# Second graph attention layer: exponentials as the stationary operand, h streaming, normalised straight from PSUM

## The chip, the cores and the metric

The kernel runs on one core of one Trainium2 chip. The metric is device time in microseconds; the kernel before took 1403.1 us (median of three runs, 1400.07 to 1413.15). Its matmuls run on TensorE, its elementwise work on VectorE, ScalarE and GpSimd, its transfers are issued mostly by SyncE. TensorE's clock is granted at one of two levels, 2.4 GHz (1.00 in the profile) or 1.2 GHz (0.50).

## The reference, cut to what matters

Four layers follow each other with residual sums: a diffusion over a graph, a top-2 mixture of experts, two graph attention layers (GAT) in a row, and a top-1 mixture of experts. The attention layers are what matters here: 1024 nodes, 8 heads, 128 channels per head in the first and 64 in the second.

```python
def gat_conv(x, src, dst, W, att_src, att_dst, bias, heads, out_ch):
    N = x.shape[0]
    h = (x @ W).reshape(N, heads, out_ch)
    a_src = jnp.einsum('nhc,hc->nh', h, att_src)
    a_dst = jnp.einsum('nhc,hc->nh', h, att_dst)
    e = jax.nn.leaky_relu(a_src[src] + a_dst[dst], NEG_SLOPE)
    m = jax.ops.segment_max(e, dst, num_segments=N)
    ex = jnp.exp(e - m[dst])
    s = jax.ops.segment_sum(ex, dst, num_segments=N)
    alpha = ex / (s[dst] + 1e-16)
    msg = h[src] * alpha[:, :, None]
    out = jax.ops.segment_sum(msg, dst, num_segments=N)
    return out.reshape(N, heads * out_ch) + bias
...
h = gat_conv(x, src, dst, W1, att_src1, att_dst1, b1, HEADS, nhid)
h = jax.nn.relu(h)
out = gat_conv(h, src, dst, W2, att_src2, att_dst2, b2, HEADS, ncls)
return jax.nn.log_softmax(out, axis=1)
```

## The kernel before, in words

One function, `attend`, writes both attention layers; `final` is true for the second. The graph is dense here: `CT` holds, for each tile of 128 source nodes and all 1024 destinations, the logarithm of the number of edges. A head is worked off in eight source tiles. One head `hd` with one source tile `s` is a pair, `k = 8 * hd + s`, 64 pairs in all. Four engines each run over the pairs in their own written order and meet by semaphores:

- GpSimd adds `CT` and a row `qb` into `am`, a ring of four tiles of 128x1024 (L1461).
- ScalarE forms a relu of 128x1024 in PSUM banks 4 and 5, `RELU` (`relu`, L1474), which VectorE adds to `am` (`counted`, L1574). `RELU` is held once, so relu `k + 1` waits until VectorE has added relu `k`.
- ScalarE takes the exponential of `am` into `PT` (`exp`, L1481), again a ring of four. In its loop relu `k + 1` stands ahead of exponential `k`.
- TensorE sums the messages of the pair into PSUM. `h` has a column of ones behind the channels of each head, so that the sum of the exponentials comes out as a last column or row.
- Between the pairs VectorE takes maxima over the neighbours of each node for two or three heads ahead (`maxed`, L1568), out of a row of scores that TensorE spreads over banks 6 and 7 (`a_row`); the table `A_ROW` sets the pair ahead of which each stands. TensorE waits there for the maxima of the head before.
- Between the pairs TensorE also makes the rest of the projection `h = x W`, in ten parts set by `H_AFTER`: behind pairs (0,1), (0,3), (1,1), (1,5), (2,1), (2,5), (3,5), (4,1), (4,5), (5,1), written (head, tile). ScalarE moves each out of PSUM three pairs later (`H_MOVED`). There is none behind (5,1).

The first layer sums with `gather` (L1688): for each of eight blocks of destinations the 128x128 exponentials are the stationary operand and `h` of one head, 129 columns, streams. The result has destinations on partitions. VectorE normalises at the next head's tile 0, right behind `counted`: `normed` waits for the eight sums, adds 1e-16, takes reciprocals (L1583, L1585) and multiplies bank by bank (L1599); the next head's first gather waits for it bank by bank. TensorE then turns the result for the second layer (`turned`).

The second layer before sums with `columns` (L1701): `h`, 65 columns, is stationary, and the exponentials stream in two matmuls of 512. The result has channels on partitions, in banks 0 and 1. ScalarE copies it to `oT` (`moved`, L1488) at tile 0 of the next head, TensorE turns it by eight transposes into banks 2 and 3 (`rows`, L1712) at tile 2, and VectorE normalises it into `zo` (L1596) at tile 4. The next head's first `columns` waits for the copy. After the last head come bias and log-softmax. Each fp32 matmul stands as two records in the trace, a transpose as one.

Of the kernel before, what the change touches and what calls it, by code (L numbers as in the profile page):

```python
# [5 lines left out]
ALU = mybir.AluOpType  # L6
ACT = mybir.ActivationFunctionType
F32 = mybir.dt.float32
# [8 lines left out]
P = 128  # L17
KIB = 1024
# [5 lines left out]
def build(nc, ins, out):  # L24

    x_d, src_d, dst_d = ins["x"], ins["src"], ins["dst"]
    N, D = x_d.shape
# [19 lines left out]
    with ctx:  # L47
# [16 lines left out]
        def place(name, shape, dt, at):  # L64

            return nc.alloc_sbuf_tensor_at(name, shape, dt, offset=BASE + at)
# [1259 lines left out]
        def attend(tag, KI, CH, xT, W, W_d, v, h, bias_d, adr, qdr, final):  # L1326
# [4 lines left out]
            NBK = -(-NT // PER)  # L1331
            SLOPE = 1 / NEG_SLOPE
            PAIRS = HEADS * NT
            EVS = 1 if final else NBK

# [10 lines left out]
            def h_units(hd, s):  # L1348

                if hd < HEADS // 2:  # L1350
# [5 lines left out]
            EARLY = 5  # L1356
            FIRST = {0: ((1, 5),), 1: ((1, 6),), 2: ((1, 7),), 3: ((2, 0), (2, 1)), 4: ((2, 2), (2, 3)),
                     5: ((2, 4), (2, 5)), 6: ((2, 6), (2, 7)), 7: ((3, 0),)}
            LATER = ({0: (1,), 1: (2,), 2: (3,), 3: (4,), 5: (5, 6), 6: (7,)} if final else
                     {1: (1,), 2: (2,), 3: (3,), 4: (4, 5), 5: (6,), 6: (7,)})  # L1360

            def maxima(hd, s):
                if hd == 0:
# [12 lines left out]
            if final:  # L1376
                bias = place(tag + "_bias", [P, F], F32, 16 * KIB)
                zo = place(tag + "_zo", [P, NT, F], F32, 129 * KIB)
                zt = place(tag + "_zt", [P, 2, F], F32, 18 * KIB)
                oT = place(tag + "_oT", [CH + 1, N], F32, 201 * KIB)  # L1380
            s_ad, s_qb = [sem(f"{tag}_ad{j}") for j in range(2)], [sem(f"{tag}_qb{j}") for j in range(2)]
            s_w = [sem(f"{tag}_w{j}") for j in range(2)]
            s_q0, s_q0m = sem(tag + "_q0"), sem(tag + "_q0_moved")
# [11 lines left out]
            with nc.Block() as block:  # L1395
# [71 lines left out]
                def _(act):  # L1467
# [13 lines left out]
                        act.activation(PT[:, k % PR, :], am[:, k % RING, :], ACT.Exp, bias=as02[:, s, hd:hd + 1],  # L1481
                                       scale=1 - NEG_SLOPE).then_inc(s_exp, 1)

                    def moved(hd):
                        act.wait_ge(s_O, NT * hd + NT)

                        wait(act, s_tr, hd)
                        act.copy(oT[:], PS[0:CH + 1, 0:2, :].rearrange("p a n -> p (a n)")).then_inc(s_oT, 1)  # L1488

                    def out(hd, half):  # L1490
                        act.wait_ge(s_tr, 2 * hd + half + 1)
                        act.activation(x2T[:, hd, half * 512:(half + 1) * 512], PS[:, 3, :], ACT.Relu,
# [36 lines left out]
                    for k in range(PAIRS):  # L1529
                        hd, s = k // NT, k % NT  # L1530
                        if k + 1 < PAIRS:
                            relu(k + 1)
                        exp(k)
                        if (hd, s) in H_MOVED:
                            h_moved(H_MOVED[hd, s], 3)
                        if final and s == 0 and hd:
                            moved(hd - 1)
                        if not final and s == 6 and hd:
                            out(hd - 1, 0)
                        if not final and s == 1 and hd >= 2:  # L1540
                            out(hd - 2, 1)
                    if not final:
                        out(HEADS - 2, 1)
                        out(HEADS - 1, 0)
                        out(HEADS - 1, 1)
                    else:
                        moved(HEADS - 1)
                        for t in range(NT):
                            act.wait_ge(s_z, t + 1)
                            act.activation(zt[:, t % 2, :], zo[:, t, :], ACT.Exp, bias=nmt[:, t:t + 1],  # L1550
                                           accum_out=sq[:, t:t + 1]).then_inc(s_ze, 1)
                            act.wait_ge(s_ze, t + 1)
                        act.activation(ve[:], sq[:], ACT.Ln).then_inc(s_ln, 1)

                @block.vector
                def _(dve):
# [17 lines left out]
                        dve.tensor_tensor(am[:, k % RING, :], RELU, am[:, k % RING, :], ALU.add).then_inc(s_all, 1)  # L1574

                    def normed(hd):
                        if final:
                            dve.wait_ge(s_tr, hd + 1)
                        else:
                            dve.wait_ge(s_O, NT * hd + NT)  # L1580
                        bank = 2 if final else 0
                        O = PS[:, bank:bank + NBK, 0:PER * (CH + 1)].rearrange("p b (t c) -> p b t c", c=CH + 1)
                        link(dve.tensor_scalar(dn[:, 0:NBK * PER].rearrange("p (b t) -> p b t", t=PER), O[:, :, :, CH],  # L1583
                                               1e-16, None, ALU.add), 2 * hd + 1)
                        link(dve.reciprocal(rd[:, 0:NBK * PER], dn[:, 0:NBK * PER]), 2 * hd + 2)  # L1585
                        scale = rd[:, 0:NBK * PER].rearrange("p (b t) -> p b t", t=PER).unsqueeze(3).to_broadcast(
                            [P, NBK, PER, CH])
                        if final:
                            dst = zo[:, :, hd * CH:(hd + 1) * CH]
                        else:  # L1590

                            wait(dve, s_tr, 2 * hd)
                            dst = o1[:, 0:NBK * PER, :]
                        dst = dst.rearrange("p (b t) c -> p b t c", t=PER)
                        if final:
                            dve.tensor_tensor(dst, O[:, :, :, 0:CH], scale, ALU.mult).then_inc(s_ev, 1)  # L1596
                        else:
                            for b in range(NBK):
                                dve.tensor_tensor(dst[:, b, :, :], O[:, b, :, 0:CH], scale[:, b, :, :], ALU.mult  # L1599
                                                  ).then_inc(s_ev, 1)  # L1600

                    dve.wait_ge(s_b, 1)
                    dve.tensor_copy(ab[:].rearrange("p t h -> p (t h)"), PS[:, 3, 0:NT * 2 * HEADS]).then_inc(s_bm, 1)
# [6 lines left out]
                    for k in range(PAIRS):  # L1610
                        hd, s = k // NT, k % NT
                        counted(k)
                        if hd and s == (4 if final else 0):
                            normed(hd - 1)
                        for ahead, t in maxima(hd, s):
                            maxed(ahead, t)
                    normed(HEADS - 1)
                    if final:

                        dve.wait_ge(s_ev, HEADS * EVS)  # L1620
                        dve.wait_ge(s_bias, 16)
                        n = 2 * HEADS
                        for t in range(NT):
# [13 lines left out]
                def _(pe):  # L1637
# [53 lines left out]
                                           stop=(s == NT - 1 and d in (NT - 1, *range(PER - 1, NT, PER))))  # L1691
                        mm.then_inc(s_O, 1)

                    def columns(hd, s):

                        if s == 0:
                            wait(pe, s_oT, hd)
                        h_ready(hd, s)
                        pe.wait_ge(s_exp, NT * hd + s + 1)
                        for half in range(2):  # L1700
                            mm = pe.matmul(PS[0:CH + 1, half, :], h[:, s, hd, :],  # L1701
                                           PT[:, (NT * hd + s) % PR, half * 512:(half + 1) * 512], start=(s == 0),
                                           stop=(s == NT - 1))
                        mm.then_inc(s_O, 1)

                    def rows(hd, moved):
                        pe.wait_ge(s_oT, hd + 1)
                        wait(pe, s_ev, hd)

                        wait(pe, s_hm, moved)  # L1710
                        for d in range(NT):
                            mm = pe.transpose(PS[:, 2 + d // PER, (d % PER) * (CH + 1):(d % PER + 1) * (CH + 1)],  # L1712
                                              oT[:, d * P:(d + 1) * P], ident[0:CH + 1, 0:CH + 1])
                        mm.then_inc(s_tr, 1)

                    def turned(hd, half, moved):
                        pe.wait_ge(s_ev, EVS * (hd + 1))
                        wait(pe, s_xm, 2 * hd + half)

                        pe.wait_ge(s_hm, moved)  # L1720
                        for d in range(NT // 2):
                            mm = pe.transpose(PS[:, 3, d * P:(d + 1) * P], o1[:, half * NT // 2 + d, :], ident[:])
                        mm.then_inc(s_tr, 1)
# [23 lines left out]
                    for k in range(PAIRS):  # L1747
                        hd, s = k // NT, k % NT
                        if k in A_ROW:
                            a_row(A_ROW[k])  # L1750
                        columns(hd, s) if final else gather(hd, s)
                        if (hd, s) in H_AFTER:
                            wait(pe, s_hm, H_AFTER[hd, s])
                            if final:
                                wait(pe, s_ev, hd if s > 2 else hd - 1)
                            else:
                                wait(pe, s_xm, turns)
                            h_tile(H_AFTER[hd, s], 3)
                        if final and s == 2 and hd:
                            rows(hd - 1, h_before(hd, s))  # L1760
                        if not final and s in (3, 7) and hd:
                            turned(hd - 1, s // 7, h_before(hd, s))
                            turns += 1
                    if final:
                        rows(HEADS - 1, 2 * NT)
                    else:
                        turned(HEADS - 1, 0, 2 * NT)
                        turned(HEADS - 1, 1, 2 * NT)

# [85 lines left out]
```

## Time and profile before

| | us |
|---|---|
| median of three runs | 1403.1 |
| the profiled execution | 1406.6 |
| its span | 1404.9 |
| TensorE busy in the span | 1075.2 (77%) |
| VectorE busy | 761.8 (54%) |
| ScalarE busy | 514.6 (37%) |
| GpSimd busy | 594.8 (42%) |
| mean granted clock of TensorE | 0.871 |

The second attention layer's pairs run from about 1010 to 1215 us of the span, those of the first layer from 752 to 957. Two records of a group of instructions can overlap, so a group's busy time is not its count times its mean. What an engine waited for stands behind its idle time, as "idle <-engine tile line" of the instruction that released it. The first attention layer runs the same code with the gathers that the change puts into the second, which makes its rows a second source of durations.

### The profile page before, as it was taken

The page shows a single profiled execution, that of the slowest core. Times are in us where ns is not written, and L with a number is a line of the kernel's source. Part 1 is how long each engine was busy: PE and PEld are TensorE (multiplying, and loading weights), DVE is VectorE, ACT ScalarE, POOL GpSimd, SP SyncE. Part 2 cuts the span into 40 slices and gives each one's busy share as a digit, 9 for nine tenths or more (in the row PEclk, how much of TensorE's full clock was granted, in tenths as well). Part 3 has the DMA queues.
Part 4 walks back from the last instruction along what each step waited for, and adds up shares of the span by engine and source line. Part 5 has one row for each costly group of instructions (what it writes and reads, how often), then busy time and mean ns, then how long its engine had stood idle before and what let it go on. Part 6 is the DMA issues. An engine that isn't in the chain of part 4 may idle for free. (4 is left out here: it accounts for less than half of the span.)

```text
span 1404.9 us, 17550 instructions
## 1 busy us (share of the span) xinstructions
PE 1075.2 (77%) x5484; PEld 740.1 (53%) x5488; DVE 761.8 (54%) x1609; ACT 514.6 (37%) x710; POOL 594.8 (42%) x471
## 2 busy tenths in 40 slices
PE   3999379650999999968398888878887887533696
PEld 2444367550777777747246777763644342132463
DVE  6888465636333333333638777751777675653134
ACT  2333433220111111101236676772466667630010
POOL 1000645105555555443026876781576777402002
PEclk9999699855999999975589999999999999855796
DMA  3000000073699999643030111101011111003974
GB/s 101 0 1 0 1 0 0 1 255 122 202 298 300 303 304 302 200 148 113 0 92 16 46 46 31 46 16 65 28 45 31 45 43 40 0 9 108 336 253 158
DMA packets 112476, 144.28 MB, mean 103 GB/s; under 512 B 30184, under 2 KB 72776, under 8 KB 112408
## 3 DMA queue, kind: packets, MB, share of 16 engines
q1 hardware_dynamic: 96168, 118.47, 26.1%
q0 software_dynamic: 14080, 21.03, 4.5%
q10 hardware_dynamic: 2160, 3.93, 0.7%
q8 instruction: 35, 0.57, 0.2%
q14 instruction: 33, 0.27, 0.1%
HBM read 138.71 MB, written 29.81 MB: 120 GB/s over the span
## 5 line engine op out<-in xcount | busy, mean ns | idle before, releaser
L1461 POOL TENSOR_TENSOR am<-CT,qb 128x1024 f32<-128x1024 f32 x128 | 299.3, 2363 | 61.7 <-ACT PT L1481 37.3
L1574 DVE TENSOR_TENSOR am<-PS,am 128x1024 f32<-128x1024 f32 x128 | 156.6, 1223 | 74.8 <-ACT PS L1474 67.1
L1474 ACT ACTIVATE PS<-adb,ab 128x1024 f32<-128x1024 f32 x128 | 142.9, 1117 | 90.5 <-DVE am L1574 90.4
L1042 DVE COPY yo<-PS 128x512 f32<-128x512 f32 x79 | 54.7, 692 | 208.9 <-PE PS L980 200.6
L1568 DVE CUSTOM_DVE_ANT_0 masked<-PS,mask 128x1024 f32<-128x1024 f32 x128 | 156.1, 1220 | 19.0 <-issue 17.3
L972 PE MATMUL PS<-xgT,w1r 128*128 128x128 f32 x1264 | 155.7, 277 | 0.0
L1007 ACT ACTIVATE hT<-PS,b1T 128x128 f32<-128x128 f32 x158 | 49.5, 364 | 288.4 <-PE PS L972 250.7
L1688 PE MATMUL PS<-h,PT 128*128 128x129 f32 x1024 | 128.3, 282 | 33.0 <-ACT PT L1481 26.4
L972 PEld LDWEIGHTS PS<-xgT,w1r 128*128 128x128 f32 x1264 | 149.2, 194 | 1.2 <-issue 1.2
L980 PE MATMUL PS<-w2r,hT 128*128 128x512 f32 x316 | 148.6, 593 | 0.1
L1481 ACT ACTIVATE PT<-am,as 128x1024 f32<-128x1024 f32 x128 | 145.2, 1134 | 0.3 <-DVE am L1574 0.3
L1688 PEld LDWEIGHTS PS<-h,PT 128*128 128x128 f32 x1024 | 122.7, 196 | 41.7 <-issue 40.5
L1701 PE MATMUL PS<-PT,h 128*65 128x512 f32 x256 | 124.9, 620 | 23.5 <-ACT PT L1481 14.3
L914 POOL DMA_INDIRECT ys_scratch<-yo,r_rowsi x64 | 65.6, 1025 | 109.0 <-DVE yo L1042 98.8
L351 DVE TENSOR_SCALAR oh_src<-iota,eT 128x1024 f16 x164 | 78.8, 480 | 17.7 <-PE PS L479 11.4
L1033 DVE COPY xgT<-PS 128x512 f32<-128x512 f32 x79 | 53.9, 683 | 54.6 <-PE PS L963 52.1
L1701 PEld LDWEIGHTS PS<-PT,h 128*65 128x65 f32 x256 | 32.9, 140 | 95.7 <-issue 79.4
L963 PEld LDWEIGHTS PS<-ident,xg 128*128 128x128 f32 x316 | 39.6, 145 | 67.6 <-issue 32.8
L980 PEld LDWEIGHTS PS<-w2r,hT 128*128 128x128 f32 x316 | 54.1, 191 | 39.2 <-issue 38.7
L479 PE MATMUL PS<-oh_src,oh_dst 128*128 x328 | 73.5, 379 | 0.9 <-DVE oh_dst L353 0.3
L909 POOL DMA_INDIRECT xg<-xs_scratch,r_rowsi x64 | 65.0, 1015 | 21.2 <-issue 20.3
L172 PE MATMUL PS<-ident,xln 128*128 128x128 f32 x96 | 20.5, 389 | 66.3 <-DVE xln L153 65.9
(308 smaller groups left out, 1601.2 us busy)
## 6 DMA issues: line engine op xcount, KB each, us to landing
w1r<-in_L_ffn_W SPq DMA_DIRECT2D x79, 512.0 KB, 6.2
w2r<-in_L_ffn_W SPq DMA_DIRECT2D x79, 512.0 KB, 7.6
adb<-a_scratch SPq DMA_DIRECT2D x16, 512.0 KB, 4.1
qb<-q_scratch SPq DMA_DIRECT2D x14, 512.0 KB, 3.7
wc<-in_L_gnn_W SPq DMA_DIRECT2D x16, 256.0 KB
xg<-xs_scratch SPq DMA_DIRECT2D x15, 256.0 KB
ys_scratch<-yo ACTq DMA_DIRECT2D x15, 256.0 KB
x_res<-in_x SPq DMA_DIRECT2D x1, 2048.0 KB, 10.5
```

The source lines that it names most:

```text
L351: dve.tensor_scalar(oh_src[:, bass.ds(slot, 1), c, :], iota[:], eT[:, 0, c, bass.ds(q, 1)], None, ALU.is_equal)
L479: mm = pe.matmul(PS[:, 2 * (t % 2) + h, :], oh_dst[:, bass.ds(slot, 1), c, :], oh_src[:, bass.ds(slot, 1), c, h * 512:(h + 1) * 512], star ...
L914: pool.indirect_dma_start(ys[0:rows, :], bass.IndirectOffsetOnAxis(picked[:, e:e + 1], 0), yo[:, e % 4, :], None, bounds_check=rows - 1, o ...
L972: mm = pe.matmul(PS[:, 2 + j % 2, c * P:(c + 1) * P], w1r[:, j, k, c * P:(c + 1) * P], xgT[:, j % 2, k, :], start=(k == 0), stop=(k == KD ...
L980: mm = pe.matmul(PS[:, 4 + j % 2, :], hT[:, j % 2, c, :], w2r[:, j, c, :], start=(c == 0), stop=(c == HC - 1))
L1461: pool.tensor_tensor(am[:, k % RING, :], CT[:, s, :], qb[:, hd % 2, :], ALU.add).then_inc(s_sum, 1)
L1474: act.activation(RELU, adb[:, hd % 2, :], ACT.Relu, bias=ab[:, s, hd:hd + 1]).then_inc(s_relu, 1)
L1481: act.activation(PT[:, k % PR, :], am[:, k % RING, :], ACT.Exp, bias=as02[:, s, hd:hd + 1], scale=1 - NEG_SLOPE).then_inc(s_exp, 1)
L1568: dve.tensor_tensor_reduce(masked[:], ASB, mask[:, t, :], 1.0, -3.0e38, ALU.subtract, ALU.max, mrow[:, hd % 2, t:t + 1]).then_inc(s_max, 1)
L1574: dve.tensor_tensor(am[:, k % RING, :], RELU, am[:, k % RING, :], ALU.add).then_inc(s_all, 1)
L1688: mm = pe.matmul(PS[:, d // PER, (d % PER) * (CH + 1):(d % PER + 1) * (CH + 1)], PT[:, (NT * hd + s) % PR, d * P:(d + 1) * P], h[:, s, hd, :],
L1701: mm = pe.matmul(PS[0:CH + 1, half, :], h[:, s, hd, :], PT[:, (NT * hd + s) % PR, half * 512:(half + 1) * 512], start=(s == 0), stop=(s == ...
```

## The change

In the second layer too, TensorE uses `gather`, so with 16 records of 65 columns for a pair in place of 4 of 512; `columns`, `rows` and ScalarE's `moved` are gone with their buffer `oT`. VectorE's `normed` reads banks 0 and 1 straight, at tile 0 of the next head, and writes `zo` in two products instead of one; the maxima that stood at tile 0 stand where the first layer has them. The projections (`h_tile`) no longer wait for the normalisation.

```diff
-            EVS = 1 if final else NBK
...
-            LATER = ({0: (1,), 1: (2,), 2: (3,), 3: (4,), 5: (5, 6), 6: (7,)} if final else
-                     {1: (1,), 2: (2,), 3: (3,), 4: (4, 5), 5: (6,), 6: (7,)})
+            LATER = {1: (1,), 2: (2,), 3: (3,), 4: (4, 5), 5: (6,), 6: (7,)}
...
-                    def moved(hd):
-                        act.wait_ge(s_O, NT * hd + NT)
-
-                        wait(act, s_tr, hd)
-                        act.copy(oT[:], PS[0:CH + 1, 0:2, :].rearrange("p a n -> p (a n)")).then_inc(s_oT, 1)
...
-                        if final and s == 0 and hd:
-                            moved(hd - 1)
...
                     def normed(hd):
-                        if final:
-                            dve.wait_ge(s_tr, hd + 1)
-                        else:
-                            dve.wait_ge(s_O, NT * hd + NT)
-                        bank = 2 if final else 0
+                        dve.wait_ge(s_O, NT * hd + NT)
+                        bank = 0
...
-                        if final:
-                            dve.tensor_tensor(dst, O[:, :, :, 0:CH], scale, ALU.mult).then_inc(s_ev, 1)
-                        else:
-                            for b in range(NBK):
-                                dve.tensor_tensor(dst[:, b, :, :], O[:, b, :, 0:CH], scale[:, b, :, :], ALU.mult
-                                                  ).then_inc(s_ev, 1)
+                        for b in range(NBK):
+                            dve.tensor_tensor(dst[:, b, :, :], O[:, b, :, 0:CH], scale[:, b, :, :], ALU.mult
+                                              ).then_inc(s_ev, 1)
...
-                        if hd and s == (4 if final else 0):
+                        if hd and s == 0:
                             normed(hd - 1)
...
-                    def columns(hd, s):
-
-                        if s == 0:
-                            wait(pe, s_oT, hd)
-                        h_ready(hd, s)
-                        pe.wait_ge(s_exp, NT * hd + s + 1)
-                        for half in range(2):
-                            mm = pe.matmul(PS[0:CH + 1, half, :], h[:, s, hd, :],
-                                           PT[:, (NT * hd + s) % PR, half * 512:(half + 1) * 512], start=(s == 0),
-                                           stop=(s == NT - 1))
-                        mm.then_inc(s_O, 1)
-
-                    def rows(hd, moved):
-                        pe.wait_ge(s_oT, hd + 1)
-                        wait(pe, s_ev, hd)
-
-                        wait(pe, s_hm, moved)
-                        for d in range(NT):
-                            mm = pe.transpose(PS[:, 2 + d // PER, (d % PER) * (CH + 1):(d % PER + 1) * (CH + 1)],
-                                              oT[:, d * P:(d + 1) * P], ident[0:CH + 1, 0:CH + 1])
-                        mm.then_inc(s_tr, 1)
...
-                        columns(hd, s) if final else gather(hd, s)
+                        gather(hd, s)
                         if (hd, s) in H_AFTER:
                             wait(pe, s_hm, H_AFTER[hd, s])
-                            if final:
-                                wait(pe, s_ev, hd if s > 2 else hd - 1)
-                            else:
+                            if not final:
                                 wait(pe, s_xm, turns)
                             h_tile(H_AFTER[hd, s], 3)
-                        if final and s == 2 and hd:
-                            rows(hd - 1, h_before(hd, s))
...
-                    if final:
-                        rows(HEADS - 1, 2 * NT)
-                    else:
+                    if not final:
                         turned(HEADS - 1, 0, 2 * NT)
                         turned(HEADS - 1, 1, 2 * NT)
```

On TensorE, from the last score row on (L1656 before, L1638 after, for head 7, in head 4), the first eight rows before (L1701 `columns`, L1673 projections, L1712 transposes; the counts are matmuls):

```order
L1656 MATMUL PS<-a_6351,sel 128x512 x2
L1701 MATMUL PS<-PT,h_8616 65x512 x2
L1673 MATMUL PS<-W2t_8618,x2T 128x128 x16
L1701 MATMUL PS<-PT,h_8616 65x512 x8
L1673 MATMUL PS<-W2t_8618,x2T 128x128 x16
L1701 MATMUL PS<-PT,h_8616 65x512 x2
L1712 MATMUL PS<-ident,a_oT 128x65 x8
L1701 MATMUL PS<-PT,h_8616 65x512 x16
```

and after, up to the end of the layer (L1670 gathers, L1655 projections):

```order
L1638 MATMUL PS<-a_6351,sel 128x512 x2
L1670 MATMUL PS<-h_8616,PT 128x65 x8
L1655 MATMUL PS<-W2t_8618,x2T 128x128 x16
L1670 MATMUL PS<-h_8616,PT 128x65 x32
L1655 MATMUL PS<-W2t_8618,x2T 128x128 x16
L1670 MATMUL PS<-h_8616,PT 128x65 x176
```

Behind the last projection nothing but gathers of 65 columns stands in TensorE's row, 176 of them, which are 22 pairs; before, matmuls of 512 columns and transposes stood there.

On VectorE, the last maximum (made in head 5) and what follows up to the end of head 6, before (L1574 is `counted`, L1583, L1585 and L1596 are `normed`):

```order
L1568 ISA masked,mrow<-PS,mask 128x1024
L1568 ISA mrow 128x1
L1574 TENSOR_TENSOR am<-PS,am 128x1024 x6
L1583 TENSOR_SCALAR dn<-PS 128x8
L1585 RECIPROCAL rd<-dn 128x8
L1596 TENSOR_TENSOR a_zo<-PS,rd 128x8x64
L1574 TENSOR_TENSOR am<-PS,am 128x1024 x8
```

and after (L1562 is `counted`, L1568, L1570 and L1581 are `normed`):

```order
L1556 ISA masked,mrow<-PS,mask 128x1024
L1556 ISA mrow 128x1
L1562 TENSOR_TENSOR am<-PS,am 128x1024 x2
L1568 TENSOR_SCALAR dn<-PS 128x8
L1570 RECIPROCAL rd<-dn 128x8
L1581 TENSOR_TENSOR a_zo<-PS,rd 128x4x64 x2
L1562 TENSOR_TENSOR am<-PS,am 128x1024 x8
```

The normalisation of head 5 has moved from behind six sums to behind two, that is from the fifth sum of head 6 to its first, and its product is made in two halves.

## Rows read from the trace of the kernel before

**Rows 1.** Second layer by head: stretch, length, busy time (records) per engine, clock
```profile
1036.60:1066.40 29.80, 24.21 (x106) 12.46 (x106) 21.63 (x39) 19.20 (x20) 25.70 (x16) 0.94 0.15 36
...
1096.10:1121.00 24.90, 19.34 (x75) 8.40 (x74) 19.98 (x35) 18.70 (x18) 18.33 (x13) 1.00 0.14 43
...
1150.80:1175.40 24.60, 18.97 (x73) 8.03 (x72) 16.08 (x26) 18.49 (x18) 14.95 (x11) 1.00 0.12 39
1175.40:1195.80 20.40, 15.74 (x40) 4.41 (x40) 10.77 (x12) 18.30 (x18) 17.68 (x9) 1.00 0.15 44
1195.80:1215.10 19.30, 15.54 (x40) 4.48 (x40) 8.75 (x10) 15.25 (x15) 12.71 (x6) 1.00 0.00 0
```

**Rows 2.** Timeline, second layer: start, duration, what, idle before it
```profile
1066.49 1.01 ACT L1488 COPY a_oT<-PS 65x1024 f32<-65x1024 f32 x1 [3.06 <-PE PS L1701]
...
1068.62 1.22 DVE L1574 TENSOR_TENSOR am<-PS,am 128x1024 f32<-128x1024 f32 x1 [5.75 <-ACT PS L1474]
...
1071.47 3.73 PE L1673 MATMUL PS<-W2t,x2T 128*128 128x128 f32 x32
...
1178.85 1.12 ACT L1474 ACTIVATE PS<-adb,ab 128x1024 f32<-128x1024 f32 x1 [0.29 <-DVE am L1574]
...
1181.33 1.12 ACT L1474 ACTIVATE PS<-adb,ab 128x1024 f32<-128x1024 f32 x1 [0.29 <-DVE am L1574]
```

**Rows 3.** Timeline, end of the second layer's last head
```profile
1211.50 3.62 PE L1701 MATMUL PS<-PT,h 128*65 128x512 f32 x8 [0.58 <-ACT PT L1481]
...
1216.21 0.71 PE L1712 MATMUL PS<-ident,a_oT 65*128 65x65 f32 x8 [1.10 <-ACT a_oT L1488]
...
1217.40 0.69 DVE L1596 TENSOR_TENSOR a_zo<-PS,rd 128x512 f32<-128x512 f32 x1
```

**Rows 4.** Timeline, first layer: two pairs of gathers in a row
```profile
884.38 3.73 PE L1688 MATMUL PS<-h,PT 128*128 128x129 f32 x32
```

**Rows 5.** Router matmuls by form (busy, mean ns, idle before), then their stretch with its clock
```profile
L641 PE MATMUL PS<-r_wg,xT 128*128 128x64 f32 x64 | 13.9, 422 | 5.1 <-DMA r_b2s<-in_L_ffn_b 5.1
L641 PE MATMUL PS<-r_wg,xT 128*128 128x8 f32 x64 | 13.8, 361 | 4.1 <-DMA r_b2s<-in_L_ffn_b 4.1
...
290.80:304.40 13.60, 13.60 (x64) 13.60 (x64) 4.19 (x21) 3.08 (x14) 0.00 (x0) 0.50 1.06 363
```

**Rows 6.** Stretches on TensorE alone: length, busy time (records), clock, DMA
```profile
1011.50:1018.10 6.60, 5.17 (x8) 0.50 0.07 1
...
1055.90:1059.10 3.20, 3.20 (x5) 0.50 0.01 3
1052.40:1055.70 3.30, 0.27 (x2) 1.00 0.00 0
...
775.60:782.60 7.00, 3.55 (x30) 1.00 0.10 9
```

**Rows 7.** Timeline, first layer's change from head 5 to head 6
```profile
912.01 0.17 DVE L1583 TENSOR_SCALAR dn<-PS 128x9 f32<-128x9 f32 x1 [1.94 <-PE PS L1688]
...
912.52 1.49 DVE L1599 TENSOR_TENSOR o<-PS,rd 128x384 f32<-128x384 f32 x3
...
913.22 2.02 PE L1688 MATMUL PS<-h,PT 128*128 128x129 f32 x16 [0.81 <-DVE o L1599]
...
917.50 2.02 PE L1688 MATMUL PS<-h,PT 128*128 128x129 f32 x16 [2.26 <-ACT PT L1481]
```

**Rows 8.** Timeline, first layer's last score row, in head 4
```profile
878.70 0.61 PE L1656 MATMUL PS<-a,sel 80*128 80x512 bf16 x2 [1.22 <-DVE mrow L1568]
```

**Rows 9.** First layer, heads 4 to 7: the columns of rows 1
```profile
860.60:888.10 27.50, 23.21 (x173) 21.68 (x172) 20.79 (x37) 19.38 (x20) 18.54 (x13) 1.00 0.14 39
888.10:911.90 23.80, 19.65 (x154) 18.48 (x152) 19.63 (x34) 18.53 (x19) 16.24 (x12) 1.00 0.10 35
911.90:934.70 22.80, 17.09 (x139) 15.69 (x138) 11.58 (x13) 18.46 (x19) 19.79 (x10) 1.00 0.14 35
934.70:956.60 21.90, 16.81 (x138) 15.58 (x137) 10.35 (x12) 15.56 (x16) 11.01 (x5) 1.00 0.00 1
```

More of the change, by code:

```diff
@@ L1379, in attend @@
                 zt = place(tag + "_zt", [P, 2, F], F32, 18 * KIB)
-                oT = place(tag + "_oT", [CH + 1, N], F32, 201 * KIB)
             s_ad, s_qb = [sem(f"{tag}_ad{j}") for j in range(2)], [sem(f"{tag}_qb{j}") for j in range(2)]
@@ L1546, in _ @@
                     else:
-                        moved(HEADS - 1)
                         for t in range(NT):
@@ L1618, in _ @@
                     if final:
-                        dve.wait_ge(s_ev, HEADS * EVS)
+                        dve.wait_ge(s_ev, HEADS * NBK)
                         dve.wait_ge(s_bias, 16)
@@ L1692, in gather @@
                         mm.then_inc(s_O, 1)
-                    def columns(hd, s):
-                        if s == 0:
-                            wait(pe, s_oT, hd)
-                        h_ready(hd, s)
-                        pe.wait_ge(s_exp, NT * hd + s + 1)
-                        for half in range(2):
-                            mm = pe.matmul(PS[0:CH + 1, half, :], h[:, s, hd, :],
-                                           PT[:, (NT * hd + s) % PR, half * 512:(half + 1) * 512], start=(s == 0),
-                                           stop=(s == NT - 1))
-                        mm.then_inc(s_O, 1)
-                    def rows(hd, moved):
-                        pe.wait_ge(s_oT, hd + 1)
-                        wait(pe, s_ev, hd)
-                        wait(pe, s_hm, moved)
-                        for d in range(NT):
-                            mm = pe.transpose(PS[:, 2 + d // PER, (d % PER) * (CH + 1):(d % PER + 1) * (CH + 1)],
-                                              oT[:, d * P:(d + 1) * P], ident[0:CH + 1, 0:CH + 1])
-                        mm.then_inc(s_tr, 1)
                     def turned(hd, half, moved):
-                        pe.wait_ge(s_ev, EVS * (hd + 1))
+                        pe.wait_ge(s_ev, NBK * (hd + 1))
                         wait(pe, s_xm, 2 * hd + half)
```

## The prediction

> **What bounds the kernel now.** I read the page first (its slices show TensorE busy for about eight tenths of the second attention layer, with VectorE and ScalarE close behind), then the table of stretches by head, the groups by line of the layer, the timeline around three changes of head, and last the granted clock. Let F be the moment at which TensorE has finished the eighth source tile of a head; the stretches of [rows 1] run from F to F. Heads 1, 2 and 4 take 29.7 to 29.8 us (one of the three rows stands), head 3 24.9, head 5 24.6, heads 6 and 7 20.4 and 19.3. TensorE is busy 24.2 us of 29.8 in head 1, but 15.7 of 20.4 in head 6. So the early heads, which carry projections (32 matmuls, 3.73 us [rows 2]), are bound by TensorE and by the waits around it. The late heads run at the beat of the chain relu, sum, relu on ScalarE and VectorE, 2.48 us a pair (from relu to relu [rows 2]; a pair is a head and a source tile), with TensorE waiting for each exponential. At a change of head ScalarE waits for F, copies 1.01 us, and only then forms the next relu; VectorE stands idle 5.75 us for it [rows 2].
>
> **What a pair costs TensorE, at the full clock.** Before: 4 records of 512 columns, 3.62 us for eight [rows 3], so 1.8 a pair. After: 16 records (each fp32 matmul is two), each loading 128x128 exponentials and streaming 65 columns. No row of this trace is exactly that at the full clock. The upper bound is the first layer, same stationary, 129 columns: 3.73 us for two pairs, 1.8 a pair [rows 4]. The lower bound is the turning's eight records of 65 columns, 0.71 us [rows 3], so 1.2 to 1.4 for sixteen; but those load 65 partitions in the transposing form. I take 1.8, because the stationary operand and number format are those of the first layer. What decides it is that loads set the spacing: in the router 64 records of 64 columns take 13.9 us and 64 records of 8 columns 13.8 [rows 5], so narrower streams bring nothing once the 128x128 load is behind them. At the full clock this edit thus costs nothing, and saves at most 0.5 us a pair.
>
> The Trainium skill, TensorE: Matmul & The Clock Gate, section LDWEIGHTS, says the same in other words: a load takes time by its columns, here 107 ns, an estimate of 1.7 us for a pair's sixteen. Its formula for an isolated gap would make 65 columns 30 ns and a pair 0.5 us; the router rows side with the load.
>
> **What the clock does.** This is the term on which my sum rests. Those router rows are at a granted clock of 0.50 from end to end: TensorE is 100% busy for 13.6 us with 64-column streams behind 128x128 loads and the clock never rises [rows 5]. It did rise, each time, within a few us of streams of 128 columns and more: the half-clock stretches in this layer (the shortest and the longest stand there, 3.2 and 6.6 us at 0.50) end under 512-column sums or projections [rows 6]. And it falls easily: before the stretch at 1055.9 TensorE had been busy 0.27 of 3.3 us [rows 6]. In the first layer the clock survived a change of head (7.0 us, busy 3.55, 30 matmuls, 1.00 [rows 6]) with 129-column streams. The changed layer has the same pauses and half the columns. I therefore take that the clock falls at every change of head, stays at half while only gathers run, rises during a projection, and then holds while TensorE works without pause. At half, a pair costs 16 x 0.2125 = 3.4 us, from the router's 13.6 us for 64 [rows 5]; that is above the 2.48 us beat, so TensorE becomes the bound.
>
> **Change of head, parts removed and added.** Removed: the copy (1.0 us of ScalarE), the turning (0.7 us of TensorE), the old places of the waits. Added: VectorE's normalisation now waits for F and holds back the next sum. The first layer does just this [rows 7]: from F (about 911.8) denominators at F+0.2, products from F+0.7, three of 1.49 us together, first gather at F+1.4, second at F+5.7, after 2.26 us idle for its exponential. Here there are two products of 128x256 instead of three of 128x384: I estimate 0.8 us together (0.69 for 128x512 before [rows 3], split), so all behind them comes 0.7 sooner: first gather F+1.3, second F+5.0. Queued behind the wait on VectorE are the next sum, the maxima, and through them ScalarE's relu and exponential; this is the beat lost at each change. The maxima's new places are those of the first layer and are in its rows; the projections' dropped wait costs and saves nothing, since it was for a normalisation of the head before, done us earlier, and TensorE goes from sums to projection without a pause.
>
> **The sum, by head (cold means half clock).**
> - Head 6: second gather at F+5.0, then seven at 3.4 = 23.8, and 0.2 for the last drain: 29.0, before 20.4: +8.6. Head 7: 29.0, before 19.3: +9.7. There is no projection in these heads to lift the clock.
> - Heads 1, 2, 4: second gather cold, ends F+8.4. Projection: 6.8 if all cold (32 x 0.2125), 3.7 if warm; I take 5.8, as stretches of dense work at half clock lasted 3.2 to 6.6 [rows 6]. F+14.2. Gathers 2 to 4 warm, 5.4; score row 0.5; gather 5 1.8; projection 3.7; gathers 6 and 7 3.6: 29.2. The maxima release the score row at F+17.4 (first layer 878.7, 18.1 behind the F of 860.6 [rows 8, 9], less 0.7), before TensorE reaches it, so hidden. Against 29.8, 29.7, 29.8: -1.7 together.
> - Head 3 has only the late projection: F+5.0, four cold gathers 13.6, score row 1.0, gather 3.4, projection 5.8, two gathers 3.7: 32.5, before 24.9: +7.6.
> - Head 5 has the early one only: F+14.2 and six warm gathers 10.8: 25.0, before 24.6: +0.4.
> - Head 0: the clock is at half from 1011.5 to 1018.1 before too, and rises under the 512-column sum; now the first projection meets half clock, 5.8 for 3.65 us: +2.1, less 0.6 of slack in front of the score row: +1.5.
> - End: from F to the end of the product 3.0 us before (copy, turning, denominators, product) [rows 1, 3]; after, 0.2 + 0.5 + 0.8 = 1.5: -1.5.
>
> Sum: 1.5 - 1.7 + 7.6 + 0.4 + 8.6 + 9.7 - 1.5 = +24.6 us. The profiled execution took 1406.6 us, so 1431.2; that execution lies 3.5 above the median of the three runs (1403.1), so against the median about 1428. The load of what follows is unchanged: the closing log-softmax is VectorE and ScalarE.
>
> **Rivals.**
> - *The clock holds (0.15).* Then only the order matters. The first layer gives the heads: 27.5, 23.8, 22.8, 21.9 for heads 4 (standing for 1 to 4), 5, 6, 7 [rows 9]; less 0.7 for the shorter normalisation and 0.4 for the turning and relu copies it has and this has not: 4 x 26.4 + 22.7 + 21.7 + 20.8 = 170.8 against 178.6 before. With the end, -9.3: 1394 against the median. Late heads lose 1.3 and 1.5 to the earlier wait, heads 1, 2 and 4 gain 3.4 each. For it: TensorE would never pause over 2 us. Against it: the router rows. At the lower price of a gather it would be some 5 us less again (0.5 for each gather behind a projection), 1389. The Trainium skill's page on the clock gate, section Why this matters for your kernels, warns of idle gaps between bursts as what drops the clock; by that alone, this rival is the outcome.
> - *Only the last heads fall (0.05).* Cold in 6 and 7 alone: +18.3, heads 1 to 5 as in the first rival -10.5, end -1.5: +6.3, 1409.
> - *The clock falls again after each projection (0.05).* Per head 1, 2, 4 four gathers (6.4), score row 0.4, second projection 2.1, last gathers 3.2, so +12.1 each; head 5 +9.6, head 3 +3.2, head 0 about +5: 1428 + 54 = 1482. Against it: behind a projection the gathers run without a pause.
> - *The forecast (0.75):* its own range is 1415 to 1440: six projections between 3.7 and 6.8 instead of 5.8 are -12.6 or +6, and a few us for waits of ScalarE on a late projection.
>
> **How the numbers follow.** Likeliest 1428. From 1408 (second rival) to 1442 I hold 0.8; outside stand the first and the third rival. This kernel can be told from itself to about 1%, 14 us. Faster by over 1% (below 1389) only in the lowest corner of the first rival, 0.03; within 1%: the rest of the first rival and the second, 0.17; slower: 0.80.
>
> **What would show it.** In the profile after: a granted clock near 0.5 for heads 6 and 7 and 16 records of a pair in 3.4 us; TensorE without idle there, VectorE waiting for it at the changes; head 3 over 30 us, heads 1, 2, 4 near 29; second gather 5 us behind F. I am wrong if the clock stays at 1.00 in heads 6 and 7 (then heads near 22 us), or if a warm gather takes clearly under 1.8 us.

## The result and the profile after

The changed kernel takes 1423.5 us (median of four runs, 1418.55 to 1425.95) against 1405.6 for the kernel before in the same comparison: a ratio of 1.0119, interval 1.0061 to 1.0178. It is slower, by 17.9 us. Measured again beside other kernels it was 1424.1 against 1407.8, ratio 1.0111 (1.0085 to 1.0138).

The stretches of the second attention layer by head, from one end of a head's sums on TensorE to the next, in the changed kernel; they answer to [rows 1]. The columns are the same: stretch, length, busy time with records on TensorE, its weight loads, VectorE, ScalarE and GpSimd, granted clock, DMA share, GB/s. The rows are heads 1 to 7.

```profile
1030.60:1058.50 27.90, 26.82 (x195) 26.41 (x194) 20.02 (x36) 18.15 (x18) 23.55 (x15) 0.82 0.16 39
1058.50:1086.20 27.70, 24.87 (x195) 24.50 (x194) 20.05 (x37) 18.24 (x18) 19.84 (x14) 0.88 0.14 39
1086.20:1118.20 32.00, 29.28 (x162) 28.69 (x162) 20.00 (x36) 17.88 (x17) 19.94 (x14) 0.63 0.12 34
1118.20:1146.70 28.50, 26.63 (x194) 26.21 (x194) 20.05 (x37) 18.14 (x18) 19.83 (x13) 0.82 0.14 38
1146.70:1170.60 23.90, 22.88 (x160) 22.61 (x160) 18.86 (x33) 17.77 (x17) 15.82 (x13) 0.79 0.15 45
1170.60:1199.50 28.90, 26.10 (x129) 25.83 (x128) 10.83 (x13) 17.50 (x16) 22.73 (x10) 0.57 0.09 28
1199.50:1228.30 28.80, 27.76 (x128) 27.46 (x128) 9.60 (x11) 14.27 (x13) 7.10 (x3) 0.50 0.00 1
```

Against 29.8, 29.7, 24.9, 29.8, 24.6, 20.4 and 19.3 before, heads 1, 2, 4 and 5 are a little shorter, head 3 is 7.1 longer, and heads 6 and 7 are 8.5 and 9.5 longer. The clock column tells why: 0.57 and 0.50 where it had been 1.00. TensorE's timeline shows pairs at both rates, projections under a rising clock, and at the end the pairs of head 5 behind its projection and those of heads 6 and 7:

```profile
1082.45 3.68 PE L1670 MATMUL PS<-h,PT 128*128 128x65 f32 x32
...
1090.86 13.89 PE L1670 MATMUL PS<-h,PT 128*128 128x65 f32 x64 [1.71 <-ACT PT L1478]
...
1108.70 5.95 PE L1655 MATMUL PS<-W2t,x2T 128*128 128x128 f32 x32
...
1126.34 5.68 PE L1655 MATMUL PS<-W2t,x2T 128*128 128x128 f32 x32
...
1154.81 5.12 PE L1655 MATMUL PS<-W2t,x2T 128*128 128x128 f32 x32
1159.77 10.83 PE L1670 MATMUL PS<-h,PT 128*128 128x65 f32 x96
1171.64 1.97 PE L1670 MATMUL PS<-h,PT 128*128 128x65 f32 x16 [1.04 <-DVE a_zo L1581]
1175.33 24.13 PE L1670 MATMUL PS<-h,PT 128*128 128x65 f32 x112 [1.71 <-ACT PT L1478]
1200.50 27.81 PE L1670 MATMUL PS<-h,PT 128*128 128x65 f32 x128 [1.05 <-DVE a_zo L1581]
```

Two pairs take 3.68 us at the full clock and four take 13.89 at half, 1.84 and 3.47 a pair. Six pairs in a row behind a projection keep the full clock (10.83, 1.8 each). The last 15 pairs, 24.13 and 27.81 us, never return to it. TensorE by itself, around the change to head 3 and from head 6 on (length, busy, clock, DMA):

```profile
1082.50:1089.20 6.70, 5.60 (x49) 1.00 0.00 0
1089.40:1113.20 23.80, 22.34 (x103) 0.50 0.15 45
1174.80:1228.30 53.50, 51.89 (x240) 0.50 0.05 16
```

VectorE at the change from head 5 to head 6, which answers to [rows 7] (TensorE's gathers there are the ones at 1171.64 and 1175.33 above), and at the end, which answers to [rows 3]:

```profile
1170.64 0.17 DVE L1568 TENSOR_SCALAR dn<-PS 128x8 f32<-128x8 f32 x1 [2.93 <-PE PS L1670]
...
1228.35 0.17 DVE L1568 TENSOR_SCALAR dn<-PS 128x8 f32<-128x8 f32 x1 [11.65 <-PE PS L1670]
1228.55 0.20 DVE L1570 RECIPROCAL rd<-dn 128x8 f32<-128x8 f32 x1
1228.79 0.75 DVE L1581 TENSOR_TENSOR a_zo<-PS,rd 128x256 f32<-128x256 f32 x2
```

The span of this execution is 1416.7 us, only 11.8 above the one before, although the layer costs more than that. The difference lies in a stage that the change does not touch, ahead of the attention layers, where weights are loaded and folded. It ran 54 us in the execution before (first row) and 47 in that of the changed kernel (second row):

```profile
622.00:676.00 54.00, 46.43 (x198) 40.37 (x197) 23.77 (x35) 10.09 (x21) 20.91 (x20) 0.50 0.44 138
```

```profile
622.00:669.00 47.00, 45.99 (x200) 40.88 (x199) 31.05 (x35) 10.09 (x21) 20.57 (x19) 0.50 0.48 160
```

So spans of single executions are compared here by stretches of the layer, whole times by medians.

### The profile page after: what moved, and what is told of

Its sections match the earlier page's. It is cut to its first block and busy times, and to the rows that moved or that the text cites. A ratio compares the mean times of both kernels' runs of the same rounds, so it can differ in the third digit from the quotient of the medians.

```text
span 1416.7 us, 18940 instructions
## 1 busy us (share of the span) xinstructions
PE 1118.3 (79%) x6192; PEld 870.2 (61%) x6192; DVE 769.6 (54%) x1617; ACT 507.5 (36%) x702; POOL 594.8 (42%) x471
## 5 line engine op out<-in xcount | busy, mean ns | idle before, releaser
L1670 PE MATMUL PS<-h,PT 128*128 128x129 f32 (+1 forms) x2048 | 292.9, 309 | 48.9 <-ACT PT L1478 36.6
L1670 PEld LDWEIGHTS PS<-h,PT 128*128 128x128 f32 x2048 | 285.4, 224 | 61.3 <-issue 59.2
L1562 DVE TENSOR_TENSOR am<-PS,am 128x1024 f32<-128x1024 f32 x128 | 156.5, 1222 | 51.0 <-ACT PS L1471 44.7
L963 PE MATMUL PS<-ident,xg 128*128 128x128 f32 x316 | 50.2, 284 | 26.6 <-DMA xg<-xs_scratch 23.2
L1655 PE MATMUL PS<-W2t,x2T 128*128 128x128 f32 (+1 forms) x384 | 68.3, 345 | 0.0
```

What stands on the lines that cost most here:

```text
L963: mm = pe.transpose(PS[:, j % 2, k * P:(k + 1) * P], xg[:, j % 4, k * P:(k + 1) * P], ident[:])
L1655: mm = pe.matmul(PS[:, bank, columns_out], xT[:, k, tile * P:(tile + 1) * P], W[half][:, k, columns_in], start=(k == 0), stop=(k == KI - 1))
L1670: mm = pe.matmul(PS[:, d // PER, (d % PER) * (CH + 1):(d % PER + 1) * (CH + 1)], PT[:, (NT * hd + s) % PR, d * P:(d + 1) * P], h[:, s, hd, :],
```

## The experiments

**The changed kernel again.**

> The changed kernel again, beside the others. Every theory: about 1.012 of the kernel before, heads 1 to 7 of the second layer 197.6 us together as in its first profile, heads 6 and 7 at a granted clock of 0.5.

Ratio 1.0111. Heads 1 to 7 took 197.6 us once more, with the clock at half for the last 54. Its stretches of heads 1 to 7 are within 0.1 us of those above. (The first four kernels here were measured beside runs of the kernel before with a median of 1407.8 us, the last four beside others with 1408.8.)

**Wide streams.** TensorE's loads and number of instructions stay as in the changed kernel, and so does the order, but each gather of the second layer streams `h` twice. The sums then lie in three banks instead of two, so VectorE's product comes in three parts instead of two, 0.82 us instead of 0.76.

```diff
-            PER = min(512 // (CH + 1), 4)
+            WC = 2 * (CH + 1) if final else CH + 1
+            PER = min(512 // WC, 4)
...
+                            dst = PS[:, d // PER, (d % PER) * WC:(d % PER + 1) * WC]
+                            rhs = h[:, s, hd, :]
+                            if final:
+                                dst = dst.rearrange("p (a c) -> p a c", c=CH + 1)
+                                rhs = h[:, s, hd:hd + 1, :].to_broadcast([P, 2, CH + 1])
```

> The changed kernel, except that each gather of the second layer streams h twice (130 columns in place of 65), into three banks in place of two; same 128x128 loads, same number of instructions, same waits. Clock theory (narrow streams let the clock fall and do not lift it): the clock stays at 1.00 through the heads, as in the first layer; heads 1 to 4 about 26.4 us each, heads 5, 6, 7 22.7, 21.7, 20.8, so 171 us for heads 1 to 7 and 26 us less than the changed kernel, some 9 less than the kernel before (0.993). Rival A (the sixteen loads or the number of instructions cost the time): no faster than the changed kernel, 1.012 or above. Rival B (VectorE's wait at the change of head costs it): also 1.012, clock at any level.

Measured: 1396.5 us, ratio 0.9928 (0.9900 to 0.9955). Its stretches for heads 1, 3, 5, 6 and 7:

```profile
1034.00:1060.70 26.70, 22.52 (x194) 21.86 (x194) 20.14 (x38) 19.55 (x20) 25.87 (x17) 1.00 0.16 42
1087.30:1115.60 28.30, 21.23 (x163) 19.85 (x162) 20.13 (x38) 17.88 (x17) 21.02 (x14) 0.94 0.14 38
1142.20:1165.10 22.90, 19.06 (x161) 18.24 (x160) 18.96 (x34) 17.50 (x17) 16.08 (x12) 1.00 0.12 41
1165.10:1186.90 21.80, 16.19 (x128) 14.88 (x128) 10.93 (x14) 17.53 (x17) 20.24 (x10) 1.00 0.15 43
1186.90:1207.90 21.00, 15.95 (x128) 14.81 (x128) 9.67 (x13) 14.52 (x14) 10.44 (x5) 1.00 0.01 1
```

Twice the columns, and 27.6 us less in median than the changed kernel. The clock stays at 1.00, although TensorE's pauses at a change of head are the same as before (0.99 and 1.79 us; 1.05 and 1.71 in the changed kernel), and heads 6 and 7 take 21.8 and 21.0, where 21.7 and 20.8 were worked out from the first layer. All seven together take 173.9 us, 171 were expected. The loads and the order were not what cost the time; rivals A and B both fall. Only head 3 still loses 1.6 us, to one half-clock stretch (0.94): TensorE waits there 2.86 us for the maxima that release the score row, as the first layer does in its head 3.

Wide streams do not make a fall impossible. In the first layer of this same execution, where 129 columns stream, the clock fell behind four changes of head, though it had held at those four in the trace of [rows 9]. It came back under the gathers alone, and heads 5 to 7 grew no longer for it (head 4 by 0.3 us). Head 6 of the first layer, then TensorE by itself in it (length, busy, clock, DMA):

```profile
907.70:930.40 22.70, 18.09 (x138) 17.07 (x137) 11.56 (x13) 18.37 (x19) 20.53 (x10) 0.92 0.13 31
```

```profile
913.40:916.40 3.00, 3.00 (x15) 0.50 0.07 5
```

That head takes 22.7 us with this stretch and took 22.8 at 1.00 in [rows 9]. With 65 columns the gathers had not lifted the clock in 53.5 us.

**An idle projection behind (6,1) and (7,1).** More work, added in the heads that have none to lift the clock.

```diff
                             h_tile(H_AFTER[hd, s], 3)
+                        if final and (hd, s) in ((6, 1), (7, 1)):
+                            h_tile(2 * NT - 1, 3)
```

> The changed kernel with 32 more records of work: the last projection is made again, its result unused, behind pairs (6,1) and (7,1). Clock theory: a projection lifts the clock and back-to-back gathers then hold it, so heads 6 and 7 become like head 5, 23.9 us in place of 28.9 and 28.8: 9.9 us faster than the changed kernel (1.005 of the kernel before), although it does more. Rivals A and B: each added projection takes TensorE 3.7 us in heads where it is never idle, so heads 6 and 7 become 32.6 us, 7 us slower (1.017).

Measured: 1414.4 us (median of twelve runs, 1406.5 to 1423.1), ratio 1.0054 (1.0027 to 1.0081), 9.8 less than the changed kernel. Heads 5, 6 and 7, then TensorE in head 6:

```profile
1151.80:1175.80 24.00, 22.88 (x160) 22.61 (x160) 18.92 (x34) 17.78 (x17) 15.93 (x13) 0.79 0.15 45
1175.80:1199.70 23.90, 21.17 (x160) 20.95 (x160) 10.80 (x13) 17.51 (x16) 22.05 (x10) 0.86 0.10 34
1199.70:1223.60 23.90, 21.15 (x160) 20.94 (x160) 9.59 (x11) 14.28 (x13) 7.73 (x4) 0.86 0.00 1
```

```profile
1180.45 3.65 PE L1670 MATMUL PS<-h,PT 128*128 128x65 f32 x16 [1.71 <-ACT PT L1478]
1183.90 5.09 PE L1655 MATMUL PS<-W2t,x2T 128*128 128x128 f32 x32
1188.82 10.83 PE L1670 MATMUL PS<-h,PT 128*128 128x65 f32 x96
```

The gather ahead of the projection is at half (3.65), the projection ends the half-clock stretch, and the six gathers behind it are at full. Unused work made each of the heads 5 us shorter. Both halves of the clock step are shown: what lifts it, and that gathers without a pause then hold it.

**Half the load.** Each gather loads 64 columns of exponentials in place of 128, which leaves out the sums of half the destinations.

```diff
-                            mm = pe.matmul(PS[:, d // PER, (d % PER) * (CH + 1):(d % PER + 1) * (CH + 1)],
-                                           PT[:, (NT * hd + s) % PR, d * P:(d + 1) * P], h[:, s, hd, :],
+                            PL = 64 if final else P
+                            mm = pe.matmul(PS[0:PL, d // PER, (d % PER) * (CH + 1):(d % PER + 1) * (CH + 1)],
+                                           PT[:, (NT * hd + s) % PR, d * P:d * P + PL], h[:, s, hd, :],
```

> The changed kernel, but each gather of the second layer loads 64 of the 128 columns of exponentials and so leaves out the sums of half the destinations; 65 columns stream as before, same number of instructions. Step on the price of a pair (the load sets the spacing, not the stream or the instruction): at the full clock a record takes about 0.06 us in place of 0.11, a pair 1.0; at half clock a pair 1.75 us, below the beat of 2.48, so heads 6 and 7 take about 22 us although the clock is at 0.5. If the spacing is set by something per instruction: records stay at 0.11 and 0.21 us and heads 6 and 7 at 28.9.

One execution took 1390.8 us. Heads 6 and 7, and three single pairs, the first at the full clock, the others at half:

```profile
1154.60:1176.10 21.50, 14.76 (x128) 13.55 (x128) 10.77 (x12) 17.37 (x17) 19.93 (x10) 0.58 0.16 45
1176.10:1196.00 19.90, 13.39 (x128) 12.42 (x128) 9.61 (x11) 14.69 (x14) 10.67 (x5) 0.62 0.00 0
```

```profile
1171.64 1.12 PE L1671 MATMUL PS<-h,PT 128*64 128x65 f32 x16 [0.59 <-ACT PT L1478]
...
1177.13 1.97 PE L1671 MATMUL PS<-h,PT 128*64 128x65 f32 x16 [1.05 <-DVE a_zo L1581]
1180.82 1.97 PE L1671 MATMUL PS<-h,PT 128*64 128x65 f32 x16 [1.72 <-ACT PT L1478]
```

A single pair at half clock takes 1.97 us in place of 3.65, and at the full clock 1.12 in place of 1.97, with the same 65 columns and the same 16 records: the load sets the spacing. And although the clock is at half for most of these heads, they take 21.5 and 19.9, since 1.97 is below the beat of 2.48 us. A low clock costs only where it lifts TensorE above the beat. The clock was not at 0.50 throughout, as had been expected: with nothing but these gathers on TensorE it rose once in head 6 and twice in head 7. Behind loads of 128 the same 65 columns had not lifted it. What about the shorter load does this, no run here shows.

**No normalisation at the last changes of head.** The wide kernel, in which neither VectorE nor TensorE waits at the changes to heads 6 and 7.

```diff
-                        if hd and s == 0:
+                        if hd and s == 0 and not (final and hd in (6, 7)):
                             normed(hd - 1)
...
-                                wait(pe, s_ev, NBK * (hd - 1) + d // PER + 1)
+                                wait(pe, s_ev, NBK * (min(hd, 5) - 1 if final else hd - 1) + d // PER + 1)
```

> The wide kernel, with the normalisation of heads 5 and 6 left out (their results are set to zero ahead of the last normalisation), so that neither VectorE nor TensorE waits at the changes to heads 6 and 7. Theory on the order (VectorE's wait for the last gather costs the late heads about 2 us each at the full clock): heads 6 and 7 fall from 21.8 and 21.0 us to the beat of the chain, eight times 2.48, 19.8 us, or 19 for the last. If the wait is hidden: both stay within 0.3 us of 21.8 and 21.0.

One execution took 1389.1 us. From the end of head 4 to the end of head 7 the layer took 61.9 us; in the wide kernel 65.7 (22.9 + 21.8 + 21.0). VectorE keeps the beat over the change from head 5 to head 6, 1154.18 to 1156.71 to 1159.19, without the pause:

```profile
1154.18 1.22 DVE L1563 TENSOR_TENSOR am<-PS,am 128x1024 f32<-128x1024 f32 x1
1156.71 1.22 DVE L1563 TENSOR_TENSOR am<-PS,am 128x1024 f32<-128x1024 f32 x1 [1.31 <-ACT PS L1472]
1159.19 1.22 DVE L1563 TENSOR_TENSOR am<-PS,am 128x1024 f32<-128x1024 f32 x1 [1.25 <-ACT PS L1472]
```

The sum at 1156.71 is head 6's first; the normalisation would stand behind it. So the early wait costs 3.8 us over two changes, 1.9 each, as the theory on the order had it. It is a real price of the change, but hidden behind the clock's in the changed kernel.

**Normalise one sum later.** VectorE forms the sum that ScalarE needs next while TensorE is still at the last gather, and normalises then.

```diff
-                        if hd and s == 0:
+                        if hd and s == (1 if final else 0):
                             normed(hd - 1)
```

> The wide kernel, with the second layer's normalisation behind the second sum of the next head in place of the first. Theory (the beat is lost since VectorE waits for TensorE before it may form the sum that ScalarE needs next): VectorE makes that sum while TensorE still gathers, then normalises; the second gather follows the first without a pause; late heads 19.9 us in place of 21.8 and 21.0, early ones 1 to 1.5 us shorter each: 9 us less than the wide kernel, 0.987 of the kernel before. Rival (the first gather, which now starts 0.5 us later, sets the head): no gain or 0.5 us a head lost, 0.993 to 0.996.

Measured on the wide kernel: 1391.1 us, ratio 0.9879 (0.9849 to 0.9909); 9 us less than the wide kernel were expected, 5.4 were found, and 5.5 in the seven stretches. Heads 2, 5, 6 and 7, then the change from head 5 to head 6:

```profile
1059.30:1086.30 27.00, 23.94 (x194) 23.38 (x194) 20.12 (x37) 18.04 (x18) 21.47 (x15) 0.94 0.14 40
1140.30:1161.80 21.50, 18.79 (x160) 18.16 (x160) 18.37 (x34) 15.24 (x15) 14.30 (x11) 1.00 0.13 42
1161.80:1181.70 19.90, 15.95 (x129) 14.81 (x128) 10.90 (x14) 17.51 (x17) 18.20 (x9) 1.00 0.17 48
1181.70:1200.90 19.20, 15.74 (x129) 14.74 (x128) 9.05 (x12) 14.62 (x14) 12.40 (x6) 1.00 0.01 1
```

```profile
1161.17 1.23 DVE L1563 TENSOR_TENSOR am<-PS,am 128x1024 f32<-128x1024 f32 x1 [1.26 <-ACT PS L1472]
...
1162.31 0.16 DVE L1569 TENSOR_SCALAR dn<-PS 128x9 f32<-128x9 f32 x1
...
1163.26 3.81 PE L1680 MATMUL PS<-h,PT 128*128 128x130 f32 x32 [1.43 <-DVE a_zo L1577]
```

TensorE is done with head 5 at 1161.8, while VectorE still forms the sum; the denominators come right behind it, with no idle time, and the first two gathers run as one piece of 32 records. Heads 6 and 7 take 19.9 and 19.2, 0.5 and 0.1 less than before the change (20.4 and 19.3), and 1.9 and 1.8 less than in the wide kernel. The early heads did not gain what was expected: 26.8 us in head 1 and 27.0 in heads 2 and 4, where the wide kernel has 26.7, and only head 3 fell, from 28.3 to 27.0. Heads 5 to 7 carry nearly all of the gain. The clock took the rest back, as head 2 shows:

```profile
1075.10 0.72 PE L1643 MATMUL PS<-a,sel 80*128 80x512 bf16 x2 [2.07 <-DVE mrow L1557]
1075.61 3.53 PE L1680 MATMUL PS<-h,PT 128*128 128x130 f32 x16
```

The score row comes 15.8 us behind the start of the head, 1.3 earlier than in the wide kernel. But TensorE has waited 2.07 us for it instead of 1.37, the clock falls right behind that wait, and the next gather takes 3.53 us instead of 1.95. From the score row to the end of the head it is 11.2 us, where the wide kernel takes 9.6.

**The same in both layers.** The edit of the kernel above, with `if hd and s == 1` for either layer.

> The same in both attention layers. Theory: the first layer has the same change of head and loses about 2 us at each late one; another 6 to 10 us less, 0.981. Rival: its turning and relu copies are late then and give it back, 0.987.

Measured: 1383.4 us, ratio 0.9840 (0.9808 to 0.9872), the fastest of all kernels here: some 40 us below the changed one, 25 below the one before. Against the kernel above, the first layer's last two heads went from 22.8 and 21.9 to 20.5 and 19.7; of its five others three gained 1.3 to 1.5 and two stayed within 0.2. Together its seven stretches are 8.6 us shorter, which agrees with the 7.7 us between the medians of this kernel and the one above; their intervals overlap, so the stretches are the better evidence.

**The later normalisation on the changed kernel.** The edit of "Normalise one sum later", at 65 columns.

> The changed kernel (65 columns) with the second layer's normalisation behind the second sum. Clock theory: at half clock TensorE is the bound and runs without a pause from the first gather, so heads 6 and 7 stay at 28.5 to 29 us. Rival B (VectorE's wait is what costs in the changed kernel): they fall by 2 us and more.

One execution took 1423.1 us, within the changed kernel's range. Heads 1 to 5 are together 3.0 us shorter than in the changed kernel, which one time cannot resolve. Heads 6 and 7:

```profile
1170.90:1199.50 28.60, 27.54 (x128) 27.38 (x128) 10.84 (x13) 18.42 (x17) 23.89 (x11) 0.50 0.10 29
1199.50:1228.10 28.60, 27.54 (x128) 27.38 (x128) 8.39 (x11) 12.09 (x11) 4.73 (x2) 0.50 0.00 1
```

TensorE is busy 27.54 of 28.60 us at 0.50. An edit worth 1.9 and 1.8 us a head at the full clock is worth 0.3 and 0.2 here: at half clock TensorE alone is the bound, and what VectorE waits for is TensorE.

Where the edit takes the second pause away, the clock can hold: it fell at the changes to heads 1, 3 and 4, but stayed at 1.00 over those to heads 2 and 5, where TensorE paused once, for 1.05 and 1.04 us. In head 5 it then fell in the middle of the head, just behind pauses of 0.67 and 0.51 us:

```profile
1161.84 1.97 PE L1670 MATMUL PS<-h,PT 128*128 128x65 f32 x16 [0.67 <-ACT PT L1478]
1164.32 6.55 PE L1670 MATMUL PS<-h,PT 128*128 128x65 f32 x32 [0.51 <-ACT PT L1478]
```

So with 65 columns a change of head is not the only place where the clock falls.

## Why the prediction was right, point by point

- **The clock falls at every change of head and stays at half under gathers alone.** Right. It fell behind six of the seven changes, and at the seventh it was at half already: 0.50 for the last 53.5 us, 97% of them busy. The wide kernel and the idle projection show it from both sides. By the Trainium skill's rule on idle gaps alone (TensorE: Matmul & The Clock Gate, section Why this matters for your kernels) the clock should have held. TensorE's longest pause at these changes was 1.71 us, and at the changes to heads 1 and 5 the clock fell in the first pause already, 1.05 us long, so the router's rows [rows 5] were the better guide. One premise was weaker than it looked: that the clock survives the changes of the first layer at 129 columns held in the trace before and in that of the changed kernel, and did not in the first layer of the wide kernel.
- **A pair costs 1.8 us at the full clock, 3.4 at half.** Right: 1.84 and 3.47, read over two and four pairs. That the load sets this and not the stream was argued from the router's rows; the kernel with half the load shows it, at both clocks.
- **Heads 6 and 7: 29.0 each.** 28.9 and 28.8. Head 3: 32.5, measured 32.0. Head 0: +1.5, measured +1.4 (27.9 from the first gather, 26.5 before).
- **Heads 1, 2, 4: 29.2; head 5: 25.0.** Too long: 27.9, 27.7, 28.5 and 23.9. Two terms were mis-sized. Projections under a rising clock were put at 5.8 us; the five in these heads and head 3 took from 4.83 to 5.95, 5.3 in the mean. And behind F, the end of the head before on TensorE, first and second gather stand at F+1.0 and F+4.7, not F+1.3 and F+5.0; the second ended at F+8.2, not F+8.4.
- **The end: -1.5.** From the last sum to the last product 1.24 us in place of 2.97: -1.7.
- **The sum: +24.6.** In the profiled layer +18.9: head 0 +1.4, heads 1 to 7 +19.2 (197.7 against 178.5), end -1.7. The medians differ by 17.9 and 16.3. Of the 5.7 too many, 4.6 lie in heads 1, 2, 4 and 5: 3.1 in the projections (counted to the start of what follows), 0.9 in the earlier end of the second gather, the rest in work at the full clock priced 0.2 too high a head. The other 1.1 lie in the other heads and the end. The measured 1423.5 us stands 4.5 below the 1428 forecast and inside the range. It came that close by some luck: the kernel before measured 2.5 us higher in this comparison than at the time of the forecast, so the difference was missed by 6.7. It is just beyond the 1% from which it was to be called slower, and the interval, 1.0061 to 1.0178, reaches to both sides of that line.
- **The rival in which the clock holds** was priced at 1394 with heads of 26.4, 22.7, 21.7 and 20.8. The wide kernel stands in for that rival, with twice the columns: 1396.5, heads 26.7, 22.9, 21.8, 21.0, and 28.3 for head 3, which the rival put at 26.4 since it took head 4 of the first layer for all of heads 1 to 4. Against the kernel before it is 11.3 us shorter; 9.3 were worked out. Its loss of 1.3 and 1.5 in the late heads is measured at 1.4 and 1.7.
- **The other two rivals** did not happen: the clock fell in the early heads too, and did not fall again between a projection and the end of a head.

## What to carry to other kernels

Before swapping the stationary and the streaming operand, look at what remains of the stream: a narrow stream behind a full load costs no more per pair at the full clock, but it can leave TensorE at half clock even when it is hardly idle, and then it becomes the bound. Where columns are free behind the load, streaming something twice can be cheaper than streaming it once. And an engine that must wait for the end of a stage should first do the one step that another engine needs next: here that was worth 1.8 to 1.9 us in each of the last two heads with wide streams, and 2.3 in those of the first layer. Look at the next wait too: in the early heads the clock took most of it back there.

## What was not expected of the hardware

That the same gathers twice as wide would be worth some 26 us, that unused matmuls would pay for themselves (28.9 us without, 23.9 with), and that a clock at half is harmless under the beat of the other engines (21.5 us at a granted clock of 0.58 with half the load, 21.8 at 1.00 in the wide kernel) all stood in the expectations. Three things did not. Gathers of 65 columns lifted the clock once their loads were half as long. With 65 columns and full loads the clock fell just behind pauses of 0.67 and 0.51 us in one kernel, and held over one of 1.05 us elsewhere in it. And the first layer, which no edit but the one in both layers touches, kept the full clock over four changes of head in some executions and lost it for a few us in others, at a cost of at most 0.4 us a head.
